# Recurrence on one core: the input products of a tile spread over thirteen steps instead of eight

## The chip, the cores and the metric

The kernel runs on one core of one Trainium2 chip. The metric is the device time of one execution in microseconds (us); lower is better.

## What is computed

Two residual blocks on x of 4 x 512 x 256 (batch B, time T, width D), all float32. The second one holds nearly all the time:

```python
# block 0: x = x + L0(x); L0 is a low-rank adapted two-layer MLP, adapted by cond_1024
# block 1: x = x + L1(x)
xW = jnp.einsum('ntd,dh->nth', x, Wx) + b
def step(prev_h, xw_t):
    next_h = jnp.tanh(xw_t + prev_h @ Wh)
    return (next_h, next_h)
_, hs = jax.lax.scan(step, h0, jnp.swapaxes(xW, 0, 1))   # h0 = cond_1024
```

The scan has 512 steps, each of which needs the state of the one before.

## The kernel before

Block 0 takes the first 80 us and leaves its result in `x2T`, with D on the partitions. Then `over_pairs` runs 16 pairs of two tiles; a tile is 16 time steps (`TS`), a pair 32 (`PAIR`). A step number s below counts within the pair; "step 8 of a tile" is s % 16 == 8.

float32 matrices are written as sums of bfloat16 parts: Wh and Wx as three parts each (`whp`, `wxp`), the state h as a high part, a residue `r_ring` and a last part `l_ring`, and x as three parts (`xp`). One step works like this:

- **TensorE** (L642, `product`) adds 24 small products to the two PSUM banks of the step: 12 with the high part of h, 8 with `r_ring`, 4 with `l_ring`. Each is a weight load of 128 x 128 and a matmul of 32 columns. The products of half m = 0 end first and raise `z_ready`, those of m = 1 follow.
- **ScalarE** (ACT, L349) takes tanh of each half into `h_ring` and raises `h_ready`.
- **VectorE** (DVE, L469 and L473) makes `r_ring` and `l_ring` of it for the next step. TensorE meanwhile starts on the high part.

The part that does not depend on the state, x times Wx plus b, is put into the banks one tile ahead: while tile p runs, the four banks of the other tile (`zbank(1 - p, q, m)`, q for even and odd steps, m for the half) get their **input products** (L617 for b, L622 for x): 1 + 2 x 6 = 13 for each bank, 52 in a tile, each again a weight load and a matmul of 32 columns. In each step they stand behind the step's 24 products in TensorE's queue, and ahead of the next step's. Before the change they begin at step 8 (`PREFETCH`): seven in steps 8, 10, 12 and 14, six in steps 9, 11, 13 and 15, none in steps 0 to 7. Tile 0 gets its own ahead of the recurrence, and there are none in the last tile, so this happens in 31 tiles.

The parts `xp` of the next tile are made in the first steps of the current one: ACT L324 after step 0, DVE L442 and ACT L328 in step 1, DVE L447 in step 2, which raises `xp3_ready`. Once per pair, from the second on, TensorE turns the finished outputs `y_sb` (two float32 transposes, L631, in steps 4 and 5, `TURN`) into the upper half of bank `zbank(1, 0, 0)`, from where ACT moves them to `o_sb` after step 5 (L339, raises `o_ready`) for SyncE to store. The order on each queue is that of the program; nothing reorders it.

Of the kernel before, what the change touches and what calls it, by code (L numbers as in the profile page):

```python
# [24 lines left out]
P = 128  # L25
RANK = 8
LN_EPS = 1e-5
TS = 16
# [4 lines left out]
def adaptive_lowrank_then_recurrence(nc, x, cond, base_up, base_down, ln_gamma, ln_beta, W1, bias1, W2,  # L33
                                     bias2, Wx, Wh, b_rnn, out):
    B, T, D = x.shape
    K2 = D // P
# [10 lines left out]
    W = 32  # L47
# [3 lines left out]
    with ExitStack() as ctx:  # L51
        def sb(name, shape, dt=F32):
            return ctx.enter_context(nc.sbuf_tensor(name, shape, dt))

        def sem(name):
            return ctx.enter_context(nc.semaphore(name))
# [25 lines left out]
        ones = sb("ones", [P, TC // 2], BF16)  # L82
# [27 lines left out]
        wxp = [sb(f"wxp{i}", [P, K2, D], BF16) for i in range(NPART)]  # L110
# [4 lines left out]
        b3h = sb("b3h", [P, D], BF16)  # L115
        xp = [sb(f"xp{i}", [P, K2, TC], BF16) for i in range(NPART)]
# [51 lines left out]
        xp2_ready = sem("xp2_ready")  # L168
# [16 lines left out]
        def slot_before(s):  # L185
            return (s - 1) % PAIR


        SUMS, TURN, ROWS, PREFETCH = 3, 4, 5, 8

        def zbank(p, q, m):
            return bank[4 * p + 2 * q + m]
# [296 lines left out]
        def _(pe):  # L491
# [47 lines left out]
            for c in range(NCH):  # L539
                for k in range(K2):  # L540
                    pe.wait_ge(ld_w2[c][k], 16)
                    for j in range(NTYPE):
# [3 lines left out]
                                                stop=(k == K2 - 1), skip_group_check=True)  # L546
# [65 lines left out]
            PAIRS6 = [(0, 0), (1, 0), (2, 0), (0, 1), (1, 1), (0, 2)]  # L612

            def input_products(p, q, m, halves, pairs=PAIRS6):
                zb = zbank(p, q, m)[:, 0:TS // 2 * W].rearrange("p (t w) -> p t w", w=W)[:, :, 0:B]
                if halves[0] == 0 and pairs[0] == (0, 0):
                    nc.tensor.matmul(zb, b3h[:, P * m:P * (m + 1)], ones[:], start=True, stop=False,  # L617
                                     skip_group_check=True)
                for k in halves:
                    for w, v in pairs:  # L620
                        rhs = xp[v][:, k].rearrange("p (t q b) -> p t q b", q=2, b=B)[:, :, q, :]
                        nc.tensor.matmul(zb, wxp[w][:, k, P * m:P * (m + 1)], rhs, start=False, stop=False,  # L622
                                         skip_group_check=True)


            def output_transpose(done_pair, n):
                if n == 0:
                    pe.wait_ge(y_ready, 2 * done_pair + 2)
                    if not (isinstance(done_pair, int) and done_pair == 0):
                        pe.wait_ge(o_ready, done_pair)  # L630
                nc.tensor.transpose(zbank(1, 0, 0)[:, D + P * n:D + P * (n + 1)],  # L631
                                    y_sb[:, n].rearrange("p b t -> p (b t)"), ident[:]).then_inc(yT_ready, 1)

            def recurrence(pair, first, last):
                for s in range(PAIR):
                    p, q, before = s // TS, s % 2, slot_before(s)
                    col0 = W * (s % TS // 2)
                    done = 2 * PAIR * pair + 2 * s

                    def product(part, k, m, rhs, stop=False):  # L640
                        n = B if stop else W
                        return nc.tensor.matmul(zbank(p, q, m)[:, col0:col0 + n], whp[part][:, k, P * m:P * (m + 1)],  # L642
                                                rhs[:, 0:n],
                                                start=False, stop=stop, skip_group_check=True)

                    for k in range(K2):
                        pe.wait_ge(h_ready, done + k + 1)
                        for m in range(K2):
                            for part in range(NPART):
                                product(part, k, m, h_hi[:, k, before, :])  # L650
                    pe.wait_ge(r_ready, done + 1)
                    for m in range(K2):
                        for part in range(2):
                            product(part, 0, m, r_hi[:, 0, q, :])
                    pe.wait_ge(r_ready, done + 2)
                    for part in range(2):
                        product(part, 1, 0, r_hi[:, 1, q, :])
                    pe.wait_ge(l_ready, done + 1)
                    product(0, 0, 0, l_ring[:, 0, q, :])
                    pe.wait_ge(l_ready, done + 2)  # L660
                    product(0, 1, 0, l_ring[:, 1, q, :], stop=True).then_inc(z_ready, 1)
                    for part in range(2):
                        product(part, 1, 1, r_hi[:, 1, q, :])
                    product(0, 0, 1, l_ring[:, 0, q, :])
                    product(0, 1, 1, l_ring[:, 1, q, :], stop=True).then_inc(z_ready, 1)


                    if TURN <= s < TURN + K2 and not first:
                        output_transpose(pair - 1, s - TURN)
                    i = s % TS - PREFETCH  # L670
                    if i >= 0 and not (last and p == 1):
                        if i == 0:

                            pe.wait_ge(xp2_ready, 2 * pair + p + 2)
                            pe.wait_ge(xp3_ready, 2 * pair + p + 2)
                            if p == 0 and not first:
                                pe.wait_ge(o_ready, pair)
                        input_products(1 - p, i // 4, i // 2 % 2, [i % 2])
                if last:
                    for n in range(K2):  # L680
                        output_transpose(pair, n)
# [9 lines left out]
            pe.wait_ge(whp_ready, 1)  # L691
            pe.wait_ge(pad_ready, 3)
            over_pairs(recurrence)


# [22 lines left out]
```

## Time and profile before

| | us |
|---|---|
| median of three runs | 574.6 (574.06 to 574.62) |
| the profiled execution | 576.19 |
| its span, first to last instruction | 574.4 |
| TensorE busy in the span | 514.5 (90%) |
| VectorE busy | 286.4 (50%) |
| ScalarE busy | 172.9 (30%) |
| mean granted TensorE clock, share of full | 0.722 |

The profiled execution is 1.8 us longer than its span and 1.6 us above the median of the runs. TensorE's busy share counts matmuls that overlap in its pipeline, so 90% does not say that it works at its peak. The granted clock is a mean over stretches at 0.5 (1.2 GHz) and at 1.0 (2.4 GHz).

### The profile page before, as it was taken

Reading aid. Unit: us, or ns where it says so; the run is one execution under the profiler, and the core shown is the slowest. Engines: PE = TensorE matmul, PEld = TensorE weight load, DVE = VectorE, ACT = ScalarE, POOL = GpSimd, SP = SyncE. Lnnn points to the kernel's source line nnn. Section 1 sums busy time; section 2 is a strip of 40 time slices with the busy share of each in tenths; the row PEclk is TensorE's granted clock in tenths of the full one; section 3 lists DMA queues with packets and bytes.
Section 4 is the critical chain, followed back from the end, with each engine's and each line's share of the span. In section 5 each row is a group of like instructions: output and inputs, shape, how many; then the busy total and the mean of one; then the engine's idle time right before and its main releaser. Section 6 shows DMA issues by size and latency. Waiting matters only on the chain.

```text
span 574.4 us, 32005 instructions
## 1 busy us (share of the span) xinstructions
PE 514.5 (90%) x14200; PEld 438.1 (76%) x14200; DVE 286.4 (50%) x2214; ACT 172.9 (30%) x1128; POOL 17.7 (3%) x32
## 2 busy tenths in 40 slices
PE   4879989999999999999999999999999999999995
PEld 3234458888888888888888888888888888888885
DVE  2232355555555555555555555555555555555553
ACT  3021113333333333333333333333333333333322
POOL 2036000000000000000000000000000000000000
PEclk9868987777676667676767676676767768686775
DMA  7950000000000000000000000000000000000000
GB/s 260 387 180 0 0 3 4 5 13 4 13 4 14 4 13 4 13 6 12 4 6 11 5 13 3 14 5 13 3 14 3 14 4 13 3 11 7 4 13 11
DMA packets 11216, 15.99 MB, mean 28 GB/s; under 512 B 1587, under 2 KB 6978, under 8 KB 11074
## 3 DMA queue, kind: packets, MB, share of 16 engines
q1 hardware_dynamic: 11078, 13.95, 7.2%
q8 instruction: 111, 1.82, 1.3%
q14 instruction: 27, 0.22, 0.1%
HBM read 11.85 MB, written 2.10 MB: 24 GB/s over the span
## 4 chain that ended last, share of the span: by engine, by line
PE 83%; ACT 8%; SPq 3%; issue 3%; DMA 3%; DVE 0%; DVEq 0%
PE bank L642 65%; ACT h_ring L349 8%; PE bank L622 7%; PE bank L578 3%; DMA w_sb<-in_L_cond_W 3%; PE bank L590 2%; SPq L217 2%; PE bank L631 2%; PE bank L617 1%; PE bank L560 1%; PE bank L567 1%; PE bank L504 0%; PE bank L543 0%; ACT xT L303 0%; DVE x2T L435 0%
## 5 line engine op out<-in xcount | busy, mean ns | idle before, releaser
L642 PE MATMUL bank<-h_ring,whp 128*128 128x32 bf16 x6144 | 250.1, 185 | 39.9 <-ACT h_ring L349 39.7
L642 PEld LDWEIGHTS bank<-h_ring,whp 128*128 128x128 bf16 x6144 | 197.3, 101 | 83.8 <-ACT h_ring L349 59.9
L469 DVE TENSOR_TENSOR r_ring<-h_ring 128x4 f32<-128x4 f32 x1024 | 136.3, 163 | 228.7 <-ACT h_ring L349 224.9
L349 ACT ACTIVATE h_ring<-bank 128x4 f32<-128x4 f32 x1024 | 141.0, 173 | 330.2 <-PE bank L642 330.2
L642 PE MATMUL bank<-r_ring,whp 128*128 128x32 bf16 x4096 | 217.3, 184 | 0.0
L642 PEld LDWEIGHTS bank<-r_ring,whp 128*128 128x128 bf16 x4096 | 174.8, 101 | 0.0
L642 PE MATMUL bank<-l_ring,whp 128*128 128x32 bf16 (+1 forms) x2048 | 154.9, 176 | 0.0
L473 DVE TENSOR_TENSOR l_ring<-r_ring 128x4 bf16<-128x4 f32 x1024 | 135.9, 162 | 0.0
L642 PEld LDWEIGHTS bank<-l_ring,whp 128*128 128x128 bf16 x2048 | 121.5, 101 | 0.0
L622 PE MATMUL bank<-xp,wxp 128*128 128x32 bf16 x1536 | 78.9, 183 | 0.0
L622 PEld LDWEIGHTS bank<-xp,wxp 128*128 128x128 bf16 x1536 | 58.4, 100 | 0.0
L617 PE MATMUL bank<-ones,b3h 128*128 128x32 bf16 x128 | 23.5, 184 | 1.6 <-ACT xp L324 1.6
L578 PE MATMUL bank<-xT,wd 128*128 128x512 f32 x32 | 17.6, 703 | 0.8 <-DVE wd L416 0.8
L435 DVE SCALAR_TENSOR_TENSOR x2T<-xT,bank 128x512 f32<-128x512 f32 x8 | 8.6, 1073 | 16.4 <-PE bank L590 16.4
L631 PE MATMUL bank<-ident,y_sb 128*128 128x128 f32 x32 | 14.2, 450 | 0.8 <-DVE y_sb L457 0.8
L617 PEld LDWEIGHTS bank<-ones,b3h 128*128 128x128 bf16 x128 | 12.9, 101 | 2.4 <-issue 2.4
L457 DVE TENSOR_TENSOR y_sb<-x2T,h_ring 128x64 f32<-128x64 f32 x64 | 14.3, 265 | 0.6 <-ACT h_ring L349 0.6
L543 PE MATMUL bank<-w_sb,gRep 128*32 128x512 f32 x64 | 11.0, 818 | 4.0 <-DMA w_sb<-in_L_cond_W 4.0
L578 PEld LDWEIGHTS bank<-xT,wd 128*128 128x128 f32 x32 | 6.9, 225 | 9.7 <-issue 8.2
L590 PE MATMUL bank<-midT,wu 128*128 128x512 f32 x32 | 14.2, 593 | 0.0
L319 ACT ACTIVATE midT<-bank 128x512 f32<-128x512 f32 x8 | 4.8, 597 | 26.7 <-PE bank L578 26.7
L401 DVE TENSOR_TENSOR wmul<-bank,rmask 128x512 f32<-128x512 f32 x4 | 2.8, 692 | 18.5 <-PE bank L543 18.5
(80 smaller groups left out, 137.1 us busy)
## 6 DMA issues: line engine op xcount, KB each, us to landing
w_sb<-in_L_cond_W SPq DMA_DIRECT2D x8, 1024.0 KB, 13.9
x_sb<-in_x SPq DMA_DIRECT2D x4, 512.0 KB, 9.5
out<-o_sb SPq DMA_DIRECT2D x64, 32.0 KB, 1.6
w_sb<-in_L_cond_W SPq DMA_DIRECT2D x1, 256.0 KB
up_sb<-in_L_cond_base_up SPq DMA_DIRECT2D x1, 256.0 KB, 4.7
down_sb<-in_L_cond_base_down SPq DMA_DIRECT2D x1, 256.0 KB, 10.3
wh_sb<-in_L_cond_Wh SPq DMA_DIRECT2D x1, 256.0 KB
wx_sb<-in_L_cond_Wx SPq DMA_DIRECT2D x1, 256.0 KB
```

The costliest lines, as they stand in the source:

```text
L217: sp.dma_start(w2_sb[:, k, :, CH * c:CH * (c + 1)], w2v[k, :, :, CH * c:CH * (c + 1)]).then_inc(ld_w2[c][k], 16)
L349: nc.scalar.activation(h_ring[:, m, s, 0:B], zt, ACT.Tanh).then_inc(h_ready, 1)
L457: last = nc.vector.tensor_tensor(y_sb[:, k, :, TS * p:TS * (p + 1)], x2T[:, k, bass.ds(col0, TC)].rearrange("p (t b) -> p b t", b=B), h_ri ...
L469: nc.vector.tensor_tensor(r_ring[:, k, q, 0:B], h_ring[:, k, before, 0:B], h_hi[:, k, before, 0:B], ALU.subtract).then_inc(r_ready, 1)
L473: nc.vector.tensor_tensor(l_ring[:, k, q, 0:B], r_ring[:, k, q, 0:B], r_hi[:, k, q, 0:B], ALU.subtract).then_inc(l_ready, 1)
L543: last = nc.tensor.matmul(bank[c][Q * j:Q * (j + 1), :], gRep[:, k].rearrange("p b r -> p (b r)"), w2_sb[:, k, j, CH * c:CH * (c + 1)], st ...
L578: last = nc.tensor.matmul(bank[4 + 2 * (b % 2) + m][:], wd[:, b, k, P * m:P * (m + 1)], xT[:, k, b, :], start=(k == 0), stop=(k == K2 - 1))
L590: last = nc.tensor.matmul(bank[2 * (b % 2) + n][:], wu[:, b, k, P * n:P * (n + 1)], midT[:, b % 2, k, :], start=(k == 0), stop=(k == K2 - 1))
L617: nc.tensor.matmul(zb, b3h[:, P * m:P * (m + 1)], ones[:], start=True, stop=False, skip_group_check=True)
L622: nc.tensor.matmul(zb, wxp[w][:, k, P * m:P * (m + 1)], rhs, start=False, stop=False, skip_group_check=True)
L631: nc.tensor.transpose(zbank(1, 0, 0)[:, D + P * n:D + P * (n + 1)], y_sb[:, n].rearrange("p b t -> p (b t)"), ident[:]).then_inc(yT_ready, 1)
L642: return nc.tensor.matmul(zbank(p, q, m)[:, col0:col0 + n], whp[part][:, k, P * m:P * (m + 1)], rhs[:, 0:n], start=False, stop=stop, skip_ ...
```

## The change

The input products begin at step 3 of a tile, four to a step, up to step 15. All 52 are issued as before, in the same 31 tiles. The order of the banks is turned: (q, m) = (0, 1), (1, 0), (1, 1) and at last (0, 0), the bank that the output transposes use; the wait for `o_ready` moves with it to the 40th product (step 12). The wait for `xp2_ready` goes, since `xp3_ready` comes after it.

```diff
-        SUMS, TURN, ROWS, PREFETCH = 3, 4, 5, 8
+        SUMS, TURN, ROWS, PREFETCH, PER_STEP = 3, 4, 5, 3, 4
...
+            BANKS = [(0, 1), (1, 0), (1, 1), (0, 0)]
+            PER_BANK = 1 + K2 * len(PAIRS6)
+
+            def input_product(p, n):
+                q, m = BANKS[n // PER_BANK]
+                i = n % PER_BANK
+                zb = zbank(p, q, m)[:, 0:TS // 2 * W].rearrange("p (t w) -> p t w", w=W)[:, :, 0:B]
+                if i == 0:
+                    nc.tensor.matmul(zb, b3h[:, P * m:P * (m + 1)], ones[:], start=True, stop=False,
+                                     skip_group_check=True)
+                else:
+                    k, (w, v) = (i - 1) // len(PAIRS6), PAIRS6[(i - 1) % len(PAIRS6)]
+                    rhs = xp[v][:, k].rearrange("p (t q b) -> p t q b", q=2, b=B)[:, :, q, :]
+                    nc.tensor.matmul(zb, wxp[w][:, k, P * m:P * (m + 1)], rhs, start=False, stop=False,
+                                     skip_group_check=True)
...
                     i = s % TS - PREFETCH
                     if i >= 0 and not (last and p == 1):
                         if i == 0:
-
-                            pe.wait_ge(xp2_ready, 2 * pair + p + 2)
                             pe.wait_ge(xp3_ready, 2 * pair + p + 2)
-                            if p == 0 and not first:
+                        for n in range(PER_STEP * i, PER_STEP * (i + 1)):
+                            if n == 3 * PER_BANK and p == 0 and not first:
                                 pe.wait_ge(o_ready, pair)
-                        input_products(1 - p, i // 4, i // 2 % 2, [i % 2])
+                            input_product(1 - p, n)
```

TensorE's queue at the end of step 3 and the start of step 4 of a tile, before:

```order
L642 MATMUL bank<-r_ring,whp 128x32 x2
L642 MATMUL bank<-l_ring,whp 128x32
L642 MATMUL bank<-l_ring,whp 128x4
L642 MATMUL bank<-h_ring,whp 128x32 [waits h_ready]
L642 MATMUL bank<-h_ring,whp 128x32 x5
```

and in the changed kernel (its lines 634, 639, 647 and 658 are lines 617, 622, 631 and 642 of before):

```order
L658 MATMUL bank<-r_ring,whp 128x32 x2
L658 MATMUL bank<-l_ring,whp 128x32
L658 MATMUL bank<-l_ring,whp 128x4
L634 MATMUL bank<-ones,b3h 128x8x4 [waits xp3_ready]
L639 MATMUL bank<-xp,wxp 128x8x4 x3
L658 MATMUL bank<-h_ring,whp 128x32 [waits h_ready]
L658 MATMUL bank<-h_ring,whp 128x32 x5
```

Four input products and one wait now stand between step 3 and step 4.

The second place is step 4 of the second and later pairs, where the output transpose (`y_sb`) stands. Before:

```order
L642 MATMUL bank<-l_ring,whp 128x4
L631 MATMUL bank<-ident,y_sb 128x128 [waits y_ready]
L642 MATMUL bank<-h_ring,whp 128x32 [waits h_ready]
L642 MATMUL bank<-h_ring,whp 128x32 x5
L642 MATMUL bank<-h_ring,whp 128x32 [waits h_ready]
```

and now:

```order
L658 MATMUL bank<-l_ring,whp 128x4
L647 MATMUL bank<-ident,y_sb 128x128 [waits y_ready]
L639 MATMUL bank<-xp,wxp 128x8x4 x4
L658 MATMUL bank<-h_ring,whp 128x32 [waits h_ready]
L658 MATMUL bank<-h_ring,whp 128x32 x5
```

Four input products follow the transpose in steps 4 and 5. The queues of the other engines hold the same instructions in the same order.

## Rows read from the trace of the kernel before

**Rows 1.** The page: the chain of work that ended last, shares of the span by line.
```profile
PE bank L642 65%; ACT h_ring L349 8%; PE bank L622 7%; PE bank L578 3%; DMA w_sb<-in_L_cond_W 3%; PE bank L590 2%; SPq L217 2%; PE bank L631 2%; PE bank L617 1%; PE bank L560 1%; PE bank L567 1%; PE bank L504 0%; PE bank L543 0%; ACT xT L303 0%; DVE x2T L435 0%
```

**Rows 2.** Who waited for whom: total us, times, longest us.
```profile
PEld bank L642 <- ACT h_ring L349: 59.9, 234, 0.3
PE bank L642 <- ACT h_ring L349: 39.7, 233, 0.2
```

**Rows 3.** Weight loads in order of time: start us, us, group, idle before; 1.2 GHz.
```profile
301.77 0.40 PEld L642 LDWEIGHTS bank<-h_ring,whp 128*128 128x128 bf16 x12 [0.24 <-ACT h_ring L349]
...
302.41 0.10 PEld L617 LDWEIGHTS bank<-ones,b3h 128*128 128x128 bf16 x1
...
302.73 0.27 PEld L642 LDWEIGHTS bank<-h_ring,whp 128*128 128x128 bf16 x7
```

**Rows 4.** Tanh of steps 9, 12, 20 and 23 of one pair.
```profile
303.48 0.28 ACT L349 ACTIVATE h_ring<-bank 128x4 f32<-128x4 f32 x2 [0.69 <-PE bank L642]
...
306.37 0.28 ACT L349 ACTIVATE h_ring<-bank 128x4 f32<-128x4 f32 x2 [0.68 <-PE bank L642]
...
313.93 0.28 ACT L349 ACTIVATE h_ring<-bank 128x4 f32<-128x4 f32 x2 [0.68 <-PE bank L642]
...
316.81 0.28 ACT L349 ACTIVATE h_ring<-bank 128x4 f32<-128x4 f32 x2 [0.69 <-PE bank L642]
```

**Rows 5.** Tanh of steps 13, 15, 17 and 19 of that pair, in between.
```profile
307.31 0.27 ACT L349 ACTIVATE h_ring<-bank 128x4 f32<-128x4 f32 x2 [0.66 <-PE bank L642]
...
309.19 0.27 ACT L349 ACTIVATE h_ring<-bank 128x4 f32<-128x4 f32 x2 [0.67 <-PE bank L642]
...
311.11 0.28 ACT L349 ACTIVATE h_ring<-bank 128x4 f32<-128x4 f32 x2 [0.49 <-PE bank L642]
...
312.98 0.27 ACT L349 ACTIVATE h_ring<-bank 128x4 f32<-128x4 f32 x2 [0.66 <-PE bank L642]
```

**Rows 6.** Stretches: us, busy time (instructions) by engine, granted clock, DMA share, GB/s.
```profile
80.57:569.20 488.63, 448.76 (x13910) 404.88 (x13906) 260.41 (x2168) 157.85 (x1099) 0.00 (x0) 0.70 0.03 8
286.00:289.40 3.40, 3.24 (x106) 2.95 (x103) 1.54 (x14) 1.12 (x8) 0.00 (x0) 0.50 0.00 0
289.40:292.80 3.40, 3.40 (x114) 3.17 (x114) 1.73 (x16) 0.84 (x6) 0.00 (x0) 0.50 0.02 5
303.10:306.50 3.40, 3.40 (x116) 3.17 (x112) 1.48 (x13) 0.97 (x8) 0.00 (x0) 0.50 0.02 5
306.50:309.90 3.40, 3.39 (x116) 3.06 (x112) 1.85 (x16) 0.97 (x8) 0.00 (x0) 1.00 0.02 5
309.90:313.30 3.40, 2.68 (x88) 2.32 (x85) 2.24 (x18) 1.43 (x10) 0.00 (x0) 1.00 0.03 10
313.40:316.90 3.50, 3.00 (x95) 2.66 (x91) 1.65 (x15) 0.93 (x7) 0.00 (x0) 0.50 0.02 5
...
514.70:518.10 3.40, 3.06 (x102) 2.72 (x99) 1.72 (x16) 1.10 (x8) 0.00 (x0) 1.00 0.16 46
518.20:521.50 3.30, 3.30 (x113) 3.10 (x109) 1.43 (x13) 0.95 (x7) 0.00 (x0) 0.50 0.00 0
...
449.90:453.30 3.40, 3.18 (x90) 2.83 (x91) 2.22 (x18) 1.20 (x8) 0.00 (x0) 0.50 0.03 5
453.40:456.60 3.20, 2.87 (x96) 2.53 (x91) 1.38 (x13) 1.04 (x9) 0.00 (x0) 1.00 0.18 48
```

**Rows 7.** Weight loads around an output transpose, then nine transposes back to back.
```profile
298.55 0.18 PEld L631 LDWEIGHTS bank<-ident,y_sb 128*128 128x128 f32 x1
298.87 0.13 PEld L642 LDWEIGHTS bank<-h_ring,whp 128*128 128x128 bf16 x2
...
34.72 1.94 PEld L504 LDWEIGHTS bank<-ident,x_sb 128*128 128x128 f32 x9
```

**Rows 8.** DVE makes the third part of x in step 2; PEld ends step 3.
```profile
296.36 0.28 DVE L447 TENSOR_TENSOR xp<-x_res,xp 128x128 bf16<-128x128 f32 x1
...
297.53 0.13 PEld L642 LDWEIGHTS bank<-l_ring,whp 128*128 128x128 bf16 x2
```

## Prediction

> **What bounds the kernel now.** I began with the chain of work that ended last [rows 1]. It puts 65% of the span on the state products (L642), 8% on tanh (L349) and 7% on the input products (L622). 7% of 574 us is 40 us, and a reader may hope to save some of it. But the chain follows TensorE's queue backwards: it also passes through work that only fills a time in which TensorE would have waited. So the next view is the waits [rows 2]: in 233 of the 512 steps TensorE waits for tanh before it can start, 39.7 us for matmuls and 59.9 us for weight loads, 0.17 and 0.26 us a time. Those are steps without input products; in the others TensorE's rows show no wait.
>
> The weight loads show how much room there is [rows 3]. Twelve loads take 0.40 us with 0.10 us for the last one, so they follow each other at (0.40 - 0.10) / 11 = 0.027 us. Behind the step's last load the first input product starts at 302.41, and the next step's first load, which waits for tanh, starts at 302.73: 0.32 us. Seven input products need 7 x 0.027 = 0.19 us of it. All of them are hidden already, with 0.13 us to spare.
>
> The test is the step time itself, from tanh to tanh, with and without input products, **at equal clock**. At 1.2 GHz steps 9 to 11, with six or seven, take (306.37 - 303.48) / 3 = 0.963 us each, and steps 20 to 22, which have none, (316.81 - 313.93) / 3 = 0.960 us [rows 4]. At 2.4 GHz steps 13 and 14 take 0.940 us with them, and 17 and 18 take 0.935 us without [rows 5]; the clocks of these stretches are in [rows 6]. So a step costs the same with none or seven of them. What bounds a step is the loop tanh, products, tanh, and what changes its length is TensorE's clock: 0.963 against 0.938 us on average, 0.025 us a step.
>
> The clock moves all the time [rows 6]. Its mean over the recurrence (488.6 us) is 0.70, so it is at 2.4 GHz for (0.70 - 0.5) / 0.5 = 0.40 of it, 195 us. A microsecond spent at 2.4 GHz in place of 1.2 does the work of 0.963 / 0.938 = 1.027, so these 195 us save 195 x 0.027 = 5.3 us. They follow the dense steps: after 303.10 to 306.50 (dense steps, 112 weight loads in the row) the clock rises; through 306.50 to 309.90 (dense, 112) it stays; after 309.90 to 313.30 (bare steps) it falls [rows 6].
>
> **The change, part by part.** *Input products taken from steps 8 to 15.* Each of these loses two or three of 0.027 us from a room that was not full. Worth nothing: the step times above say so. The most that rows allow is 0.963 - 0.960 and the rounding of the tanh rows, 0.01 us over three steps: 0.006 us x 8 steps x 31 tiles = 1.5 us, which I keep as an end.
>
> *Four input products put into steps 3 to 7.* 4 x 0.027 = 0.11 us in 0.32 us of room: hidden by the wait for tanh, as seven are in step 8. If that room were gone, 5 x 31 x 0.11 = 17 us would show.
>
> *The wait for the third part of x in step 3.* Behind it are queued step 4's products, so it could delay the loop. DVE ends that part at 296.36 + 0.28 = 296.64, and step 3's last weight loads start at 297.53 [rows 8]. It is 0.9 us early, nothing. The wait for the moved output now stands at step 12, with the copy made in step 5: nothing.
>
> *Steps 4 and 5, where the output transpose stands too.* The transpose's load starts at 298.55 and the next step's first at 298.87, 0.32 us of room [rows 7]. Back to back, such transposes come every 1.94 / 9 = 0.216 us at 1.2 GHz [rows 7]. With four input products, 0.216 + 0.108 = 0.324 us: just full. There are 15 x 2 = 30 such steps. Lower end 0; upper end all four exposed, 30 x 0.108 = 3.2 us. I take 0.1 us in all, since need and room agree to 0.004 us, and at 2.4 GHz there is more room.
>
> *The clock.* This is the term that decides. With seven or six products a step TensorE issues 30.5 pairs of load and matmul in 0.963 us, bare 24, and now 28 in 13 steps out of 16. In a stretch of 3.4 us that is 98.9 at 1.2 GHz, and a windows row counts about four more that had begun before it: 103. A row with such a mixture exists: 286.00 to 289.40, where two bare steps are followed by full ones, has 103, and the clock stayed at 1.2 GHz behind it (289.40) [rows 6]. At 2.4 GHz 28 in 0.938 us make 101.5 and with the four 105; the rows near it are 514.70 to 518.10 with 99, behind which the clock fell, and 306.50 to 309.90 with 112, behind which it stayed [rows 6]. The trace of before has no long stretch of four a step, so the bounds are: never at 2.4 GHz, and always. The nearest row at 1.2 GHz has the same density and says "stays low"; at 2.4 GHz four a step lies a little nearer to the row that fell. So steps with four products alone should seldom raise the clock.
>
> What should raise it are the transposes: in 449.90 to 453.30 bare steps with the two transposes did it alone (the next row is at 1.00) [rows 6], and now eight input products stand with them. So I expect one stretch at 2.4 GHz in each pair from about step 6, as long as the one seen from 306.50 to 313.30, 6.8 us [rows 6], and now and then a short one elsewhere. 6.8 us of a pair of 30.7 us (489 / 16 = 30.5) is 0.22, so 108 us in place of 195. 87 us less at 2.4 GHz cost 87 x 0.027 = 2.3 us.
>
> The page "TensorE: Matmul & The Clock Gate" of the Trainium skill (Part 1, and its closing table) ties a fall of the clock to idle gaps of microseconds between bursts of matmuls. This trace does not agree: the longest wait of TensorE for tanh is 0.3 us [rows 2], and the clock falls at 313.3 all the same [rows 6]. By the page's rule the clock would stay up in both kernels and this term would be nothing.
>
> **Sum.** 0 + 0 + 0 + 0.1 + 2.3 = 2.4 us more: 576.19 becomes 578.6 in the profiled execution. That execution is 1.6 us above the median of the runs shown; on the median, 574.6 + 2.4 is 577.0. The recurrence's mean clock would be 0.5 + 0.5 x 0.22 = 0.61 instead of 0.70.
>
> **The rivals.** *Four a step keep the clock up* (ends on the other side). It decides if what raises or holds the clock lies below 28 pairs in a step. Then only steps 0 to 2 of a tile are bare, too few to bring it down for long. With 0.75 of the recurrence at 2.4 GHz: (0.75 - 0.40) x 489 x 0.027 = 4.6 us less, 570.0; with half of that gain, 572.3; always high, 0.60 x 489 x 0.027 = 7.9 less, 566.7. For it: 28 is nearer to 30.5 than to 24. Against it: the row of 286.00. The page's sentence that sustained activity releases the clock speaks for this one. Chance 0.14.
>
> *The clock's share stays about as it is.* The stretch behind the transposes holds until step 3 of the next tile, which 105 against 99 and 112 allows at 2.4 GHz; steps 6 to 18 are 12 us of 30.7, again 0.40. Then nothing changes: 574.0 to 575.6. That the change does nothing because the moved work was hidden anyway also ends here. Chance 0.20.
>
> *Never at 2.4 GHz.* All 5.3 us are lost: 579.9. Against it are the transposes. Chance 0.06.
>
> *The crowded steps 4 and 5 show.* Half of the upper end, 1.6 us, on top of the forecast's clock term: 578.5. It decides once transpose and products need more than 0.32 us. Chance 0.10.
>
> *The dense steps do give something back.* 1.5 us less at an unchanged clock, 573.1. The equal step times speak against it. Chance 0.03.
>
> **How the numbers follow.** The forecast, 576.0 to 578.0, has 0.47. About 0.2% (1.1 us) is what a measurement of this kernel can tell from no change. Slower by more: 0.47 + 0.06 + 0.10 and 0.02 of the edge of the second rival, 0.65. Faster by more: 0.14 + 0.03 = 0.17. The rest, 0.18, is within. The range of 8 in 10 reaches from the milder form of the first rival, 572.3, to the crowded steps with a little more, 579.0; outside are the strong forms of the first rival and the last 0.06.
>
> **What would show it.** Right: steps 8 to 15 as long as before at equal clock; TensorE's wait for tanh shorter each time but seen in nearly all steps; mean clock of the recurrence near 0.61, with the stretches at 2.4 GHz starting behind steps 4 and 5 of a pair and few in its second tile. Wrong: a mean clock of 0.70 or more; steps 4 and 5 longer than 0.97 us at 1.2 GHz; a wait of TensorE for VectorE in step 3; or a shorter step at equal clock.

## The result and the profile after

| | before | after |
|---|---|---|
| median, us | 573.58 (570.99 to 574.85, 13 runs) | 577.56 (574.56 to 578.41, 13 runs) |
| ratio after / before, 95% interval | | 1.0062 (1.0042 to 1.0081) |
| profiled execution, us | 576.19 | 576.61 |
| span, us | 574.4 | 574.7 |
| recurrence, first to last tanh, us | 488.63 | 491.21 |
| mean granted clock in the recurrence | 0.70 | 0.65 |

The change makes the kernel 0.62% slower, 3.6 us by the ratio (the two medians differ by 4.0 us). In the profiled executions the recurrence lost 2.6 us; the first 80 us, which the change does not touch, happened to take 78.33 us in the second one instead of 80.57, so the spans hide most of the loss. Steps are compared from here on, not spans.

The page of the changed kernel: its chain of work, the answer to [rows 1].

```profile
PE bank L658 66%; ACT h_ring L349 8%; PE bank L639 6%; PE bank L578 3%; SPq L217 3%; PE bank L590 2%; DMA x_sb<-in_x 2%; PE bank L647 2%; PE bank L560 1%; PE bank L567 1%; PE bank L634 1%; SPq L220 0%; PE bank L622 0%; ACT xT L303 0%; DVE x2T L435 0%
```

Who waited for whom, the answer to [rows 2]:

```profile
PEld bank L658 <- ACT h_ring L349: 46.7, 226, 0.3
...
PE bank L658 <- ACT h_ring L349: 19.4, 108, 0.2
```

The chain looks the same. TensorE waits less for tanh (19.4 us of matmul wait in 108 steps, in place of 39.7 us in 233), and the kernel is slower: idle time of TensorE in this loop was no loss, and filling it no gain.

Tanh of steps 3 to 7 of the same pair that [rows 4] and [rows 5] are from, in the changed kernel (start us, duration us):

```profile
296.50 0.28 ACT L349 ACTIVATE h_ring<-bank 128x4 f32<-128x4 f32 x2 [0.67 <-PE bank L658]
297.46 0.28 ACT L349 ACTIVATE h_ring<-bank 128x4 f32<-128x4 f32 x2 [0.68 <-PE bank L658]
298.50 0.28 ACT L349 ACTIVATE h_ring<-bank 128x4 f32<-128x4 f32 x2 [0.76 <-PE bank L658]
...
299.55 0.28 ACT L349 ACTIVATE h_ring<-bank 128x4 f32<-128x4 f32 x2 [0.25 <-PE bank L658]
300.49 0.27 ACT L349 ACTIVATE h_ring<-bank 128x4 f32<-128x4 f32 x2 [0.67 <-PE bank L658]
```

Step 3 takes 0.96 us. Steps 4 and 5, which hold an output transpose and now four input products, take 1.04 and 1.05 (1.040 on average over the pairs), step 6 takes 0.94 at 2.4 GHz. Nothing like it was in the trace of before, where steps 4 and 5 took 0.964 us. TensorE's weight loads in step 4, the answer to [rows 7]:

```profile
297.37 0.18 PEld L647 LDWEIGHTS bank<-ident,y_sb 128*128 128x128 f32 x1
297.39 0.45 PEld L639 LDWEIGHTS bank<-xp,wxp 128*128 128x128 bf16 x4
297.77 0.18 PEld L658 LDWEIGHTS bank<-h_ring,whp 128*128 128x128 bf16 x4
```

and its matmuls:

```profile
297.39 0.45 PE L647 MATMUL bank<-ident,y_sb 128*128 128x128 f32 x1
297.64 0.32 PE L639 MATMUL bank<-xp,wxp 128*128 128x32 bf16 x4
297.79 0.29 PE L658 MATMUL bank<-h_ring,whp 128*128 128x32 bf16 x5
```

From the transpose's load to the next step's first load it is 297.77 - 297.37 = 0.40 us, where the room is 0.32 us: 0.08 us too much. The first input product starts 0.25 us behind the transpose, not 0.216.

The clock, the answer to [rows 6]: stretches of the changed kernel (us, busy time and instructions of PE, PEld, DVE, ACT, POOL, granted clock, DMA share, GB/s).

```profile
78.33:569.54 491.21, 456.73 (x13910) 407.38 (x13906) 260.26 (x2168) 157.98 (x1100) 0.00 (x0) 0.65 0.03 8
293.00:296.00 3.00, 2.44 (x80) 2.18 (x81) 1.90 (x17) 1.16 (x8) 0.00 (x0) 1.00 0.02 5
296.20:299.40 3.20, 3.17 (x99) 2.94 (x95) 1.79 (x15) 1.22 (x7) 0.00 (x0) 0.50 0.03 5
299.60:302.90 3.30, 3.10 (x102) 2.70 (x99) 1.72 (x16) 1.04 (x8) 0.00 (x0) 1.00 0.17 44
303.00:306.30 3.30, 3.20 (x103) 2.87 (x99) 1.43 (x13) 0.94 (x7) 0.00 (x0) 0.50 0.03 6
306.30:316.50 10.20, 9.39 (x287) 8.32 (x284) 5.83 (x48) 3.31 (x24) 0.00 (x0) 0.50 0.02 5
313.20:316.50 3.30, 3.19 (x99) 2.88 (x100) 1.82 (x16) 0.90 (x7) 0.00 (x0) 0.50 0.02 5
316.70:320.00 3.30, 3.08 (x102) 2.68 (x99) 1.54 (x14) 1.09 (x8) 0.00 (x0) 1.00 0.02 5
```

Behind the transposes (296.20 to 299.40) the clock rises, as forecast. It falls again after the four-a-step stretch 299.60 to 302.90. It also rises behind a stretch of the second tile that has only steps with four products (313.20 to 316.50), which was forecast as rare. It was not: in the whole trace the clock rises behind the transposes of all 15 pairs that have them, but stays up for 6.8 us in four of them only and for 3.4 us in eleven, 65 us together; the other 82 us at 2.4 GHz are 24 stretches of 3.4 us elsewhere, in both tiles. Over the recurrence 0.65 means 0.30 at 2.4 GHz, against 0.40 before. The drop does not belong to one execution: the mean clock of the whole kernel is 0.682 to 0.707 in the 13 runs of the changed kernel and 0.724 to 0.746 in 29 runs of the kernel before.

### The profile page after: what moved, and what is told of

The parts are those of the page before. It is cut to its first block, busy times and chain, and to the rows that moved or that the text cites. A ratio compares the mean times of both kernels' runs of the same rounds, so it can differ in the third digit from the quotient of the medians.

```text
span 574.7 us, 31974 instructions
## 1 busy us (share of the span) xinstructions
PE 521.8 (91%) x14200; PEld 439.9 (77%) x14200; DVE 286.2 (50%) x2214; ACT 172.9 (30%) x1128; POOL 17.7 (3%) x32
## 4 chain that ended last, share of the span: by engine, by line
PE 81%; ACT 8%; issue 4%; SPq 4%; DMA 2%; DVE 0%; ACTq 0%; DVEq 0%
PE bank L658 66%; ACT h_ring L349 8%; PE bank L639 6%; PE bank L578 3%; SPq L217 3%; PE bank L590 2%; DMA x_sb<-in_x 2%; PE bank L647 2%; PE bank L560 1%; PE bank L567 1%; PE bank L634 1%; SPq L220 0%; PE bank L622 0%; ACT xT L303 0%; DVE x2T L435 0%
## 5 line engine op out<-in xcount | busy, mean ns | idle before, releaser
L658 PE MATMUL bank<-h_ring,whp 128*128 128x32 bf16 x6144 | 249.7, 185 | 34.5 <-ACT h_ring L349 19.4
L639 PE MATMUL bank<-xp,wxp 128*128 128x32 bf16 x1488 | 105.6, 185 | 0.0
L639 PEld LDWEIGHTS bank<-xp,wxp 128*128 128x128 bf16 x1488 | 77.0, 104 | 1.9
L578 PE MATMUL bank<-xT,wd 128*128 128x512 f32 x32 | 16.4, 659 | 0.8 <-DVE wd L416 0.8
L590 PEld LDWEIGHTS bank<-midT,wu 128*128 128x128 f32 x32 | 6.1, 190 | 7.7 <-issue 7.7
L324 ACT CAST xp<-x2T 128x128 bf16<-128x128 f32 x32 | 9.6, 299 | 7.4 <-DVE x2T L435 7.4
```

Source lines behind the costliest of these rows:

```text
L324: nc.scalar.copy(xp[0][:], x2T[:, :, bass.ds(col0, TC)]).then_inc(xp1_ready, 1)
L578: last = nc.tensor.matmul(bank[4 + 2 * (b % 2) + m][:], wd[:, b, k, P * m:P * (m + 1)], xT[:, k, b, :], start=(k == 0), stop=(k == K2 - 1))
L590: last = nc.tensor.matmul(bank[2 * (b % 2) + n][:], wu[:, b, k, P * n:P * (n + 1)], midT[:, b % 2, k, :], start=(k == 0), stop=(k == K2 - 1))
```

## The experiments

**The tables.** All variants below, except h_last and z_before, come from one form of the changed kernel, in which two tables of 16 numbers say how many input products stand in each step of a tile; TURNED is for the tiles in which an output transpose stands in steps 4 and 5. Nothing else differs unless said. Lines 349 and 658 of the changed kernel (tanh and state products) are lines 351 and 660 in these variants, and 353 and 666 in those with fillers.

```diff
-                    i = s % TS - PREFETCH
-                    if i >= 0 and not (last and p == 1):
-                        if i == 0:
-                            pe.wait_ge(xp3_ready, 2 * pair + p + 2)
-                        for n in range(PER_STEP * i, PER_STEP * (i + 1)):
-                            if n == 3 * PER_BANK and p == 0 and not first:
+                    turned = p == 0 and not first
+                    counts = TURNED if turned else PLAIN
+                    i = s % TS
+                    if not (last and p == 1):
+                        done_n = sum(counts[:i])
+                        for n in range(done_n, done_n + counts[i]):
+                            if n == 0:
+                                pe.wait_ge(xp3_ready, 2 * pair + p + 2)
+                            if n == 3 * PER_BANK and turned:
```

**a_order: the old places, everything else new.**

```diff
+        PLAIN = [0, 0, 0, 0, 0, 0, 0, 0, 7, 6, 7, 6, 7, 6, 7, 6]
+        TURNED = [0, 0, 0, 0, 0, 0, 0, 0, 7, 6, 7, 6, 7, 6, 7, 6]
```

> The input products stand seven and six to a step in steps 8 to 15, as in the kernel before, but with the changed kernel's order of banks, its waits and its code. If the cost of the change lies in how many products stand in which step (crowded steps 4 and 5, and the clock), this takes the time of the kernel before within 0.2% and its mean granted clock (0.70 in the recurrence). If the turned order of the banks or the moved waits cost it, it is 0.4 to 0.6% slower than before, like the changed kernel.

Measured: ratio to before 1.0005 (0.9988 to 1.0023), 12 runs. The stretch of its recurrence:

```profile
79.47:566.87 487.40, 447.26 (x13910) 403.51 (x13906) 260.14 (x2168) 157.78 (x1099) 0.00 (x0) 0.70 0.03 8
```

Clock 0.70 again. So the order of the banks and the waits cost nothing that 12 runs can tell from zero (the interval is 1 us to either side), and what the change costs lies in which step holds how many products.

**b_uncrowd: nothing beside the transposes.**

```diff
+        PLAIN = [0, 0, 0, 4, 4, 4, 4, 4, 4, 4, 4, 4, 4, 4, 4, 4]
+        TURNED = [0, 0, 0, 4, 0, 0, 5, 5, 5, 5, 5, 5, 5, 5, 4, 4]
```

> As the changed kernel, but steps 4 and 5 of a pair that hold an output transpose hold no input product: in those tiles 4 in step 3, 5 in steps 6 to 13, 4 in steps 14 and 15. Theory 1 (transpose and four products do not fit into the wait for tanh): steps 4 and 5 fall from 1.04 us to 0.96 us, 30 x 0.08 = 2.4 us, and the kernel takes about 0.4% less than the changed one, 0.1 to 0.2% more than before. Theory 2 (the clock alone costs it): the time stays at 0.6% above before, since these 30 steps do not count. Five to a step may also bring more of the recurrence to 2.4 GHz; then the mean granted clock shows it and accounts for 0.027 us per us.

Measured: 1.0014 (0.9997 to 1.0031), 12 runs; 0.48% below the changed kernel by the two ratios, 2.8 us. Tanh of steps 4, 5 and 6 of the same pair:

```profile
296.26 0.28 ACT L351 ACTIVATE h_ring<-bank 128x4 f32<-128x4 f32 x2 [0.68 <-PE bank L660]
297.22 0.28 ACT L351 ACTIVATE h_ring<-bank 128x4 f32<-128x4 f32 x2 [0.68 <-PE bank L660]
...
298.18 0.28 ACT L351 ACTIVATE h_ring<-bank 128x4 f32<-128x4 f32 x2 [0.17 <-PE bank L660]
```

and its recurrence:

```profile
78.40:566.72 488.32, 456.26 (x13910) 404.71 (x13906) 260.25 (x2168) 157.70 (x1099) 0.00 (x0) 0.67 0.03 8
```

Steps 4 and 5 take 0.96 us again, 30 x 0.080 = 2.4 us. The clock is at 0.67 in place of 0.65, which is worth 0.04 x 489 x 0.024 = 0.5 us (0.960 against 0.938 us a step here, a ratio of 1.024). Theory 1 holds; theory 2, the clock alone, falls.

**c_crowd: the crowding alone, in the old kernel.**

```diff
+        PLAIN = [0, 0, 0, 0, 0, 0, 0, 0, 7, 6, 7, 6, 7, 6, 7, 6]
+        TURNED = [0, 0, 0, 0, 4, 4, 0, 0, 6, 5, 6, 5, 6, 5, 6, 5]
```

> As the kernel before (none in steps 0 to 3, 6 and 7, the rest in steps 8 to 15), but with four input products in each of steps 4 and 5, behind the output transpose where there is one, and six or five in steps 8 to 15. Theory 1: steps 4 and 5 with a transpose take 1.04 us at 1.2 GHz, 0.08 us more, 2.4 us in all, 0.4% above before if the clock stays as it was. Theory 2: those steps keep their 0.96 us; the time differs from before only by the clock.

The tables differ from this text in one thing: only the tiles with a transpose are changed; in the others the products stand as in the kernel before.

Measured: 1.0038 (1.0019 to 1.0057), 12 runs. Tanh of steps 4 to 6, and the recurrence:

```profile
295.48 0.28 ACT L351 ACTIVATE h_ring<-bank 128x4 f32<-128x4 f32 x2 [0.68 <-PE bank L660]
296.51 0.28 ACT L351 ACTIVATE h_ring<-bank 128x4 f32<-128x4 f32 x2 [0.76 <-PE bank L660]
...
297.56 0.28 ACT L351 ACTIVATE h_ring<-bank 128x4 f32<-128x4 f32 x2 [0.25 <-PE bank L660]
```

```profile
77.20:567.20 490.00, 448.50 (x13910) 405.26 (x13906) 260.08 (x2168) 157.68 (x1099) 0.00 (x0) 0.69 0.03 8
```

Step 4 takes 1.03 us, step 5 1.05 (1.040 on average over the pairs), at almost the clock of a_order: 490.00 - 487.40 = 2.6 us more. The crowding is shown from the other side, with the size that theory 1 gave.

**g_two: two products in place of four.**

```diff
+        TURNED = [0, 0, 0, 4, 2, 2, 5, 5, 5, 5, 4, 4, 4, 4, 4, 4]
```

> The changed kernel with two input products in place of four behind each output transpose (steps 4 and 5), the four taken away put one each into steps 6 to 9. The trace of the changed kernel shows 0.400 us from the transpose's load to the next step's first load, with four products of 0.027 us in it, against 0.32 us of room. With two it needs 0.347 us: steps 4 and 5 at 1.2 GHz take 0.960 + 0.025 = 0.985 us. If the extra 0.08 us came from something else than the length of the queue (a fixed cost of a transpose ahead of input products), they stay at 1.04 us.

Measured in one execution, 574.04 us: steps 4 and 5 take 0.98 and 0.99 us (0.987 on average).

```profile
295.34 0.28 ACT L351 ACTIVATE h_ring<-bank 128x4 f32<-128x4 f32 x2 [0.68 <-PE bank L660]
296.32 0.28 ACT L351 ACTIVATE h_ring<-bank 128x4 f32<-128x4 f32 x2 [0.71 <-PE bank L660]
...
297.31 0.17 ACT L351 ACTIVATE h_ring<-bank 128x4 f32<-128x4 f32 x1 [0.20 <-PE bank L660]
```

Two products cost 0.027 us and four cost 0.080, so the excess grows by 0.027 us with each product once the room is full: it is the length of the queue in front of the next step. By this count only one product would have fitted beside a transpose at 1.2 GHz; no run has one. The recurrence:

```profile
76.72:566.97 490.25, 457.62 (x13910) 408.15 (x13906) 260.68 (x2168) 158.23 (x1100) 0.00 (x0) 0.62 0.03 8
```

It is only 1.0 us shorter than that of the changed kernel, although 30 x 0.053 = 1.6 us of crowding are gone: in this execution the clock is at 0.62 in place of 0.65, which takes back 0.06 x 490 x 0.024 = 0.7 us.

**h_last: the transpose behind the products.**

```diff
-                    if TURN <= s < TURN + K2 and not first:
-                        output_transpose(pair - 1, s - TURN)
                     i = s % TS - PREFETCH
...
                             input_product(1 - p, n)
+                    if TURN <= s < TURN + K2 and not first:
+                        output_transpose(pair - 1, s - TURN)
```

> The changed kernel with the output transpose behind the four input products of steps 4 and 5 in place of ahead of them. If the excess is the turn from a float32 transpose to bfloat16 products (0.25 us to the first and 0.07 us to the second matmul behind it, against 0.027 us), it is there behind the products too, now in front of the next step: steps 4 and 5 stay between 1.00 and 1.06 us at 1.2 GHz. If only the wait between the transpose and its own followers counts and the next step's first load runs ahead of it, they fall to 0.96 to 0.99 us.

Measured in one execution, 578.97 us: steps 4 and 5 stay at 1.040 us. Its weight loads, then its matmuls, in step 4:

```profile
299.88 0.18 PEld L639 LDWEIGHTS bank<-xp,wxp 128*128 128x128 bf16 x4
299.99 0.18 PEld L647 LDWEIGHTS bank<-ident,y_sb 128*128 128x128 f32 x1
300.20 0.29 PEld L658 LDWEIGHTS bank<-h_ring,whp 128*128 128x128 bf16 x5
```

```profile
300.01 0.45 PE L647 MATMUL bank<-ident,y_sb 128*128 128x128 f32 x1
300.26 0.42 PE L658 MATMUL bank<-h_ring,whp 128*128 128x32 bf16 x8
```

The next step's load starts in time, 0.32 us behind the first of the products (299.88 to 300.20), but its matmul only 0.25 us behind the transpose's. Here a view of the weight loads alone would have called it hidden. The turn from the float32 transpose to bfloat16 work costs the same at either end of the products.

**d_fill7: the idle time filled.** Products that nobody reads (weights of the bias into the unused upper half of a bank) bring every step to 24 + 7; steps 4 and 5 with a transpose get none. The real products stand as before the change (the tables of a_order).

```diff
+            def filler(p):
+                nc.tensor.matmul(zbank(p, 1, 1)[:, D:D + W], b3h[:, 0:P], ones[:, 0:W], start=False, stop=False,
+                                 skip_group_check=True)
...
+        FILL = [7, 7, 7, 7, 7, 7, 7, 7, 0, 1, 0, 1, 0, 1, 0, 1]
+        FILL_TURNED = [7, 7, 7, 7, 0, 0, 7, 7, 0, 1, 0, 1, 0, 1, 0, 1]
```

> The kernel before with idle time filled: every step that has fewer than seven products behind its 24 gets products that nobody reads (weights of the bias, 32 columns, into an unused part of a bank) up to seven, but for steps 4 and 5 with a transpose, which get none. Nothing is computed with them. If a step costs the same with none and with seven, and the clock is what changes a step's length, the recurrence runs at 2.4 GHz nearly throughout: steps of 0.938 us, 0.60 x 489 x 0.027 = 7.9 us less than before, about 566 us, 1.4% faster. If the added products are not hidden, or write ports or banks collide, it is slower than before by up to 512 x 4 x 0.027 = 55 us. If the clock does not follow the density of TensorE's work, the time stays at that of before.

Measured: 565.02 us (564.22 to 566.93, 5 runs), ratio to before 0.985 (0.9826 to 0.9874). Its recurrence:

```profile
77.08:557.48 480.40, 479.27 (x15668) 435.58 (x15665) 257.96 (x2168) 155.76 (x1099) 0.00 (x0) 1.00 0.03 9
```

1758 more matmuls in the records, and 7.0 us less than the recurrence of a_order. TensorE stays at 2.4 GHz but for the first steps, and a step takes 0.938 us (median). It beats both kernels, computes nothing more, and shows what the clock term is worth.

**e_fill4, e_fill5, e_fill6: four, five and six in every step.** The real products stand as in the changed kernel (four a step, also beside the transposes); fillers bring every step to 24 + 4, 24 + 5 or 24 + 6, except that steps 4 and 5 with a transpose stay at 24 + 4. One of these lines stands in each:

```diff
+        FILL = [4, 4, 4, 0, 0, 0, 0, 0, 0, 0, 0, 0, 0, 0, 0, 0]
+        FILL = [5, 5, 5, 1, 1, 1, 1, 1, 1, 1, 1, 1, 1, 1, 1, 1]
+        FILL = [6, 6, 6, 2, 2, 2, 2, 2, 2, 2, 2, 2, 2, 2, 2, 2]
```

> The changed kernel with its bare steps 0 to 2 filled by four products each that nobody reads, so that every step of the recurrence holds exactly 24 + 4. If four a step do not keep TensorE at 2.4 GHz, as the row of equal density in the trace of before said, the recurrence stays mostly at 1.2 GHz: mean granted clock 0.6 to 0.7, most of the 2.4 GHz behind the transposes, time within 0.3% of the changed kernel. If four a step do keep it up, the clock goes to 0.9 or more and the time falls by 6 us or more.

> As e_fill4, but 24 + 5 in every step (24 + 4 in the steps with a transpose). In the trace of before the clock stayed down behind stretches of 29.0 load-and-matmul pairs per us and rose behind 31 and more; 29 in 0.963 us are 30.1 per us, between them. I expect a mixed clock, 0.75 to 0.95, and a time between those of the changed kernel and of d_fill7. The crowded steps 4 and 5 stay at 1.04 us where they fall at 1.2 GHz.

> As e_fill4, but 24 + 6 in every step (24 + 4 in the steps with a transpose): 31.2 pairs per us at 1.2 GHz. The clock should stay at 2.4 GHz nearly throughout, mean granted clock over 0.95, time within 0.3% of d_fill7.

Measured in one execution each: 576.06, 571.23 and 564.72 us. The recurrence of e_fill4:

```profile
77.28:569.07 491.79, 470.10 (x14345) 419.06 (x14342) 260.17 (x2168) 157.95 (x1099) 0.00 (x0) 0.68 0.03 8
```

of e_fill5:

```profile
81.50:564.50 483.00, 468.67 (x14827) 419.36 (x14823) 258.45 (x2168) 156.16 (x1100) 0.00 (x0) 0.93 0.03 8
```

and of e_fill6:

```profile
77.13:557.98 480.85, 477.47 (x15308) 429.02 (x15304) 258.28 (x2168) 155.72 (x1100) 0.00 (x0) 1.00 0.03 9
```

Mean clock 0.68, 0.93 and 1.00. Four a step in every step, without one bare step, leave TensorE at 1.2 GHz for nearly two thirds of the time, five for a seventh, six for the first steps alone. The rival of the prediction that four a step hold the clock falls. TensorE's waits for tanh are 0.2 us at most in all three. So idle gaps of microseconds, which the page "TensorE: Matmul & The Clock Gate" (Part 1) of the Trainium skill names, are not what lowers the clock here.

**f_full_crowd: the crowding at 2.4 GHz.** The changed kernel with fillers up to seven, and four products beside each transpose.

```diff
+        FILL = [7, 7, 7, 3, 3, 3, 3, 3, 3, 3, 3, 3, 3, 3, 3, 3]
+        FILL_TURNED = [7, 7, 7, 3, 0, 0, 3, 3, 3, 3, 3, 3, 3, 3, 3, 3]
```

> The changed kernel, its four products a step with the transpose in steps 4 and 5 included, with every other step filled up to seven by products that nobody reads. Theory: at 2.4 GHz transpose and four products take 0.11 + 0.10 us and fit into the 0.32 us of the wait for tanh, so steps 4 and 5 take 0.938 us like the others, and the time is that of d_fill7 (0.985 of before) within 0.2%. Rival: the crowding costs the same 0.08 us at either clock; then it is 2.4 us, 0.4%, above d_fill7.

Measured: 567.20 us, ratio 0.986 (0.9821 to 0.9898), 4 runs. Its recurrence takes 480.45 us against 480.40 in d_fill7, so the 2.4 us of the rival are not there; the work ahead of the recurrence took 2.2 us longer in this profiled execution (79.29 against 77.08). Step 4, from the transpose's load to the next step's first:

```profile
293.62 0.14 PEld L655 LDWEIGHTS bank<-ident,y_sb 128*128 128x128 f32 x1
293.65 0.30 PEld L643 LDWEIGHTS bank<-xp,wxp 128*128 128x128 bf16 x4
293.94 0.34 PEld L666 LDWEIGHTS bank<-h_ring,whp 128*128 128x128 bf16 x11
```

and tanh of steps 4 and 5:

```profile
293.72 0.27 ACT L353 ACTIVATE h_ring<-bank 128x4 f32<-128x4 f32 x2 [0.67 <-PE bank L666]
294.66 0.27 ACT L353 ACTIVATE h_ring<-bank 128x4 f32<-128x4 f32 x2 [0.66 <-PE bank L666]
```

The same queue fits into 0.32 us, and step 4 takes 0.94 us like the others (0.937 on average over steps 4 and 5 of all pairs). The crowding is a cost of the changed kernel only because it meets these steps at 1.2 GHz.

**z_before: the kernel before once more.** No edit.

> The kernel before, unchanged, profiled once more. In its first trace a step at 1.2 GHz took 0.964 us on average, in the traces of the changed kernel and of a_order 0.960 us. If that difference belongs to one execution and not to the kernel, this trace shows 0.960 us at 1.2 GHz and a recurrence of about 487.5 us, as a_order has; if it belongs to the kernel, 0.964 us and 488.6 us again.

Measured in one execution, 575.94 us, with a recurrence of 489.71 us. The expectation left out what came: neither 0.960 nor 0.964. Tanh of steps 20 and 23 of the same pair in z_before:

```profile
312.47 0.28 ACT L349 ACTIVATE h_ring<-bank 128x4 f32<-128x4 f32 x2 [0.69 <-PE bank L642]
...
315.37 0.28 ACT L349 ACTIVATE h_ring<-bank 128x4 f32<-128x4 f32 x2 [0.69 <-PE bank L642]
```

and in a_order:

```profile
312.20 0.28 ACT L351 ACTIVATE h_ring<-bank 128x4 f32<-128x4 f32 x2 [0.69 <-PE bank L660]
...
315.08 0.28 ACT L351 ACTIVATE h_ring<-bank 128x4 f32<-128x4 f32 x2 [0.68 <-PE bank L660]
```

0.967 against 0.960 us a step at the same clock. e_fill4 has 0.966 as well, b_uncrowd, c_crowd, g_two, h_last and the changed kernel 0.960, and the first trace of before goes between both levels. The kernel before alone has shown both, so the level is not set by the change. Its cause stays open; it is worth up to 300 steps x 0.007 = 2 us between executions of one kernel.

## Why the prediction was right, point by point

The forecast was 577.0 us, 2.4 us or 0.4% slower. Measured are 577.56 us and 0.62% slower. The sign and the range were right, the size in part by luck. The change itself was missed by 1.2 us; that the two times are only 0.6 us apart comes from the start, 574.6 us in the forecast and 573.58 in the later runs.

*A step costs the same with none and with seven input products; four in steps 3 to 7 are hidden.* Held. In the trace of a_order the steps with six or seven and those with none both take 0.960 us on average at 1.2 GHz, in the changed kernel so do the steps with four and no transpose, and d_fill7 puts seven into nearly every step at no cost. The 40 us on the chain of work were never to be had.

*The wait for the third part of x in step 3, the wait for `o_ready`, the order of banks: nothing.* Held; a_order has them at 1.0005 of before.

*Steps 4 and 5: 0.1 us.* This is the step that failed. It measured 30 x 0.080 = 2.4 us. The prediction took 0.216 us for a transpose from a row in which transposes follow each other (read as the twelve loads were, without the length of the last one, that row gives 0.213), and added four products: 0.324 us, "just full". In the changed kernel the same queue took 0.40 us. A float32 transpose with bfloat16 work behind it takes 0.25 us to the next matmul's start, and 0.07 more to the one behind that, in place of 0.216 and 0.027; the two differences make the missing 0.08. One of the prediction's own signs of being wrong, steps 4 and 5 longer than 0.97 us at 1.2 GHz, has come. The upper end of the term, 3.2 us, held it, and "half of the upper end" had a chance of 0.10. With room and need equal to 0.004 us, the value taken should have been in the middle of the range and not at its lower end.

*The clock: 2.3 us.* Right in direction, half in size, and wrong in where the time at 2.4 GHz lies. The share of the recurrence at 2.4 GHz fell from 0.40 to 0.30 and not to 0.22; that is 0.10 x 489 x 0.024 = 1.2 us. The stretches behind the transposes came in every pair but were mostly half as long as forecast (65 us in place of 108), and the stretches elsewhere, forecast as few, gave 82 us. "Steps with four products alone should seldom raise the clock" was wrong in this trace. What decides whether such a stretch raises the clock stays open: stretches alike in their counts did and did not (303.00 to 306.30 with 99 weight loads, 313.20 to 316.50 with 100).

*TensorE's wait for tanh, shorter each time but in nearly all steps,* did not come so: the matmuls waited in 108 steps, 0.18 us a time as before (0.17), the weight loads in 226, 0.21 us a time in place of 0.26.

*The sum.* 2.4 + 1.2 = 3.6 us. The recurrence of the changed kernel against that of a_order, both with 0.960 us a step at 1.2 GHz: 491.21 - 487.40 = 3.8 us. Against before, the ratio gives 3.6 us. Two errors of 2.3 and 1.1 us with opposite signs left an error of 1.2.

*The rivals.* Four a step do not keep the clock up (e_fill4, 0.68). "Never at 2.4 GHz" did not come. "Shares stay as they are" lay on the right side of the forecast but went too far.

*The rule of the Trainium skill* (page "TensorE: Matmul & The Clock Gate", Part 1) that the clock falls after idle gaps of microseconds would have given no change of clock. The measurement decides against it in this kernel: mean clocks of 0.70, 0.65 and 0.68 (e_fill4) with waits of 0.3 us at most.

## What to carry to other kernels

In a latency-bound loop, idle time of the engine in the loop is room to be filled only as far as the next critical instruction comes in time, and the room is to be measured at the slower clock and with the change of operand type in the queue. What work in the idle time can change is the clock: here, filling nearly every step with throwaway matmuls, up to seven, so that the granted clock stayed at 1.0, made the kernel 1.5% faster, which no placement of the real products in these runs did. And a share on the chain of work that only passes through a filled wait is no gain in sight; the step time with and without it, at equal clock, is the test.

## What was not expected of the hardware

- TensorE's clock fell in a loop in which it never waited longer than 0.3 us: with 24 + 4 products in every step the mean granted clock was 0.68, with 24 + 5 0.93, with 24 + 6 1.00.
- The turn from a float32 transpose to bfloat16 matmuls took 0.25 + 0.07 us to the first and second matmul behind it at 1.2 GHz, wherever it stood in the step. When the turn stood in front of the next step, the weight load was in time and the matmul was late.
- At 1.2 GHz a step took 0.960 us in some executions and 0.967 in others, of the same kernel too; at 2.4 GHz it took 0.938 in all of them (medians).
